# Attention row sums: all sixteen key tiles of a block summed on TensorE, behind the product with the values

## The reference

```
h = layer_norm(x) * scale + offset
q = (h @ wq) / sqrt(d);  k = h @ wk;  v = h @ wv          # 16 heads of width 32
q, k = rotary(q), rotary(k)
logits = einsum('bhik,bhjk->bhij', q, k)
a = softmax(logits, axis=-1)                              # over the 2048 keys j
y = einsum('bhij,bhjv->bhiv', a, v)
x = x + y @ wo
x = x + gelu(layer_norm(x) @ w1) @ w2
```

## Time and profile before

| | before |
|---|---|
| device time, median of 3 runs | 4409.26 us |
| device time, lowest and highest | 4403.0 and 4412.9 us |
| span of the profiled execution, first to last instruction | 4415.3 us |
| TensorE busy | 3909.2 us (89%) |
| VectorE busy | 2468.5 us (56%) |
| ScalarE busy | 1866.5 us (42%) |
| GpSimd busy | 2235.7 us (51%) |
| mean granted TensorE clock | 0.947 |

### The profile page before, as it was taken

How to read it: one execution, slowest core, us unless ns; L and a number is a source line. 1 busy time by engine, 2 the same in 40 slices (tenths; PEclk the granted TensorE clock), 3 DMA queues, 4 the chain that set the end, 5 groups by cost and what they waited for, 6 DMA issues and landing times. The chain is left out here.

```text
span 4415.3 us, 55170 instructions
## 1 busy us (share of the span) xinstructions
PE 3909.2 (89%) x19040; PEld 2452.9 (56%) x19040; DVE 2468.5 (56%) x3913; ACT 1866.5 (42%) x3553; POOL 2235.7 (51%) x1872
## 2 busy tenths in 40 slices
PE   5689999899899799899899996779989993997998
PEld 4545455355355354454454433668868882775776
DVE  4477878678787687877677763612211114333333
ACT  2246556556566466566565554321111112232222
POOL 0246767667677676777667774012212222343344
PEclk9889999999999899999999998889989996998999
DMA  6100000001000000000000003711110103011010
GB/s 211 59 17 25 18 20 20 9 25 28 9 23 18 16 25 22 11 27 8 22 23 8 3 6 115 249 61 48 49 58 20 58 29 131 15 48 38 27 55 19
DMA packets 103652, 184.72 MB, mean 42 GB/s; under 512 B 8976, under 2 KB 27920, under 8 KB 101136
## 3 DMA queue, kind: packets, MB, share of 16 engines
q1 hardware_dynamic: 103376, 181.15, 12.3%
HBM read 119.78 MB, written 61.08 MB: 41 GB/s over the span
## 5 line engine op out<-in xcount | busy, mean ns | idle before, releaser
L778 POOL TENSOR_TENSOR prob_sums<-prob_sums,probs 128x512 f32<-128x512 f32 x1152 | 1495.1, 1328 | 194.1 <-ACT probs L676 188.1
L580 DVE TENSOR_REDUCE part_max<-ps_att 128x1 f32<-128x512 f32 x2048 | 1316.7, 683 | 473.1 <-PE ps_att L463 459.5
L676 ACT ACTIVATE probs<-ps_att 128x512 f32<-128x512 f32 x2048 | 1130.1, 594 | 714.5 <-PE ps_att L445 670.2
L463 PE MATMUL ps_att<-k_stack,q_stack 96*128 96x512 f32 x2048 | 892.9, 440 | 102.0 <-DVE part_max L580 98.2
L445 PE MATMUL ps_att<-q_stack,k_stack 97*128 97x512 f32 x2048 | 897.7, 440 | 61.0 <-PEq L62 40.1
L445 PEld LDWEIGHTS ps_att<-q_stack,k_stack 97*128 97x128 f32 x2048 | 391.6, 192 | 499.9 <-ACT probs L676 376.5
L463 PEld LDWEIGHTS ps_att<-k_stack,q_stack 96*128 96x128 f32 x2048 | 401.6, 196 | 308.1 <-DVE part_max L580 221.6
L1209 POOL TENSOR_TENSOR ml_g_lo<-ml_g,ml_g_hi 128x512 fp32r<-128x512 f32 x128 | 164.9, 1288 | 788.6 <-DVE ml_g_hi L1185 788.6
L483 PE MATMUL ps_att<-probs,v_tok 128*32 128x512 f32 x4096 | 556.6, 616 | 2.3 <-ACT probs L676 2.3
L1185 DVE CAST ml_g_hi<-ml_g 128x512 fp32r<-128x512 f32 x128 | 54.7, 428 | 572.9 <-ACT ml_g L1145 572.9
L1145 ACT ACTIVATE ml_g<-ps_mlp 128x512 f32<-128x512 f32 x128 | 76.6, 599 | 586.9 <-PE ps_mlp L1224 586.9
(11 more groups left out here) (198 smaller groups left out, 5518.3 us busy)
## 6 DMA issues: line engine op xcount, KB each, us to landing
h_raw<-hS SPq DMA_DIRECT2D x128, 256.0 KB, 2.7
x_in_sb<-in_x SPq DMA_DIRECT2D x8, 1024.0 KB, 6.0
hS<-h_full SPq DMA_DIRECT2D x32, 256.0 KB, 2.8
yT<-o_sb SPq DMA_DIRECT2D x32, 256.0 KB, 2.1
po_x<-in_x SPq DMA_DIRECT2D x8, 1024.0 KB, 8.6
x<-po_x SPq DMA_DIRECT2D x8, 1024.0 KB, 6.6
h2T<-po_h SPq DMA_DIRECT2D x32, 256.0 KB, 2.1
ml_h<-h2T SPq DMA_DIRECT2D x32, 256.0 KB, 5.8
```

Source lines behind the costliest of these rows:

```text
L463: nc.tensor.matmul(mx[mx_uses % 2], t["qS"][0:S3, h, n * TB + q * P:n * TB + (q + 1) * P], t["kS"][0:S3, b, h, k * TB:(k + 1) * TB], start ...
L580: nc.vector.tensor_reduce(t["pm"][:, r, k:k + 1], mx[mx_uses % 2], AX.X, ALU.max)\
L676: nc.scalar.activation(t["p"][:, at % PR, h, :], sT[(at * G + h) % 2], ACT.Exp)\
L778: nc.gpsimd.tensor_tensor(t["acc"][:, h, :], x, t["p"][:, at % PR, h, :], ALU.add)\
```

## The change

All sixteen key tiles of a block are summed on TensorE, each right behind the product of the same tile with the values. The last matmul of tile 15 closes the sum. GpSimd has no additions of `probs` left; its other work stays. `last_sums` and the buffer `prob_sums` are gone. ScalarE waits, before it overwrites a `probs` buffer, for the sums of three steps ago and for nothing else, and copies the sums out right behind the values, in step 0 of the next block and not in step 2.

```diff
-POOL_SUMS = (0, 1, 2, 4, 5, 7, 8, 10, 11, 13, 14)
-PE_SUMS = tuple(k for k in range(LT) if k not in POOL_SUMS)
...
             def sums(w):
                 n, k = w // LT, w % LT
-                if k == PE_SUMS[0] and n:
+                if k == 0 and n:
                     pe.wait_ge(s["l_kept"], n)
                 for h in range(G):
                     mm = nc.tensor.matmul(l_ps[h * KD:(h + 1) * KD, :], c["ones"][:, 0:KD], t["p"][:, w % PR, h, :],
-                                          start=(k == PE_SUMS[0]), stop=False)
+                                          start=(k == 0), stop=(k == LT - 1))
                 mm.then_inc(s["psum"], 1)
...
                         if attend and at:
                             values(at - 1)
+                            sums(at - 1)
                         turn_stacks(st)
-                if attend and at and (at - 1) % LT in PE_SUMS:
-                    sums(at - 1)
-                if attend and at >= LT and k == 1:
-                    last_sums(at // LT - 1)
...
             def exps(at, heads):
                 for h in heads:
                     if at >= PR:
-                        v = at - PR
-                        if v % LT not in PE_SUMS:
-                            act.wait_ge(s["acc_done"], added(v, h))
-                        elif h == 0:
-                            act.wait_ge(s["psum"], summed(v))
                         if h == 0:
-                            act.wait_ge(s["pv"], v + 1)
+                            act.wait_ge(s["psum"], at - PR + 1)
...
             def keep_sums(n):
-                act.wait_ge(s["sum_done"], n + 1)
+                act.wait_ge(s["psum"], LT * (n + 1))
...
                 if attend and at >= LT and at % LT == 0:
                     keep_values(at // LT - 1)
-                if attend and at >= LT and at % LT == 2:
                     keep_sums(at // LT - 1)
...
-                if attend and st["k"] in POOL_SUMS and st["k"]:
-                    for h in range(G):
...
-                        nc.gpsimd.tensor_tensor(t["acc"][:, h, :], x, t["p"][:, at % PR, h, :], ALU.add)\
-                            .then_inc(s["acc_done"], 1)
```

More of the change, by code:

```diff
@@ L41 @@
 PR = 3
-POOL_SUMS = (0, 1, 2, 4, 5, 7, 8, 10, 11, 13, 14)
-PE_SUMS = tuple(k for k in range(LT) if k not in POOL_SUMS)
-POOL_ROUNDS = len(POOL_SUMS) - 1
 STEPS = NB * LT
@@ L341, in attend_groups @@
     blocks = len(halves) * NB if attend else 0
[L343 to L351, removed]
     ends = [(at + AHEAD) // (G * TT) for at, st in enumerate(steps)
@@ L493, in sums @@
                     mm = nc.tensor.matmul(l_ps[h * KD:(h + 1) * KD, :], c["ones"][:, 0:KD], t["p"][:, w % PR, h, :],
-                                          start=(k == PE_SUMS[0]), stop=False)
+                                          start=(k == 0), stop=(k == LT - 1))
                 mm.then_inc(s["psum"], 1)
-            def last_sums(n):
-                pe.wait_ge(s["acc_done"], G * POOL_ROUNDS * (n + 1))
-                for h in range(G):
-                    mm = nc.tensor.matmul(l_ps[h * KD:(h + 1) * KD, :], c["ones"][:, 0:KD], t["acc"][:, h, :],
-                                          start=False, stop=True)
-                mm.then_inc(s["sum_done"], 1)
             def turn_stacks(st):
@@ L566, in _ @@
                 sums(len(steps) - 1)
-                last_sums(blocks - 1)
         @block.vector
@@ L823, in attention @@
             hr=sb("h_raw", [P, 2, DC, P]),
-            p=sb("probs", [P, PR, G, TB]), acc=sb("prob_sums", [P, G, TB]),
+            p=sb("probs", [P, PR, G, TB]),
             k_stk=sb("k_stk", [P, 2, G * S3]), q_stk=sb("q_stk", [P, 2, G * S3]), ra=sb("rot_a", [P, 2 * P]),
@@ L830, in attention @@
         names = ("h_in0 h_in1 h_hi h_lo proj rot_cos rot_sin rotated v_kept k_hi q_hi k_split q_split turned k_kept q_kept "
-                 "w_in0 w_in1 w_hi w_lo mx_full mx_free neg_max max_set0 max_set1 score exp pv psum acc_done sum_done "
+                 "w_in0 w_in1 w_hi w_lo mx_full mx_free neg_max max_set0 max_set1 score exp pv psum "
                  "o_kept l_kept rl y_done y_stored ones_set")
```

## The result

The changed kernel takes 4521.8 us (median of 4 runs, 4520.1 to 4524.6) where the kernel before took 4410.6 us in the same job (4 runs, 4403.0 to 4412.9). The ratio is 1.0259, with a 95% interval of 1.0245 to 1.0274: 2.6% slower. Forecast were 4520 us and a range of 4475 to 4562.

The account below looks back on a forecast made before the run. Attention was taken as bound by TensorE's own order, with holes where VectorE is late. 277 us added less removed, minus 167 given back, minus 3, plus 4 makes 111 us on the 4409 us median: 4520 us, range 4475 to 4562.

Parts of the forecast that it names:

- What is added less what is removed: TensorE in attention: 512 sets of sums added, 450 us, less separate sets removed, 173 us: 277 us.
- The 0.88 us: TensorE's cost of one set of sums directly behind another set of the same shape, the values.
- The removed term: Separate sets at step ends: 70 at 1.2 us with a projection piece behind, 122 at 0.73 without: 173 us.
- What VectorE gives back: VectorE's instructions with two SBUF inputs, no longer slowed by GpSimd's additions, give back 167 us to TensorE.
- Its split: Of the 167 us: rotations 90, divisions 33, splitting the next weights 36, smaller ones 8.
- The waits: TensorE's waits for VectorE's reductions in attention were to fall from 292 to about 125 us.
- one of my own tests: Sign of being wrong: waits for VectorE fall by more than 250 us, the time then near the one before.
- Rival 1: VectorE's delays are not GpSimd's doing, or its remaining work holds VectorE just as long: 4620 us; chance 4%.
- Rival 2: Exponentials become the new wait, 0.3 us more in some 290 steps without a piece: 4607 us; chance 8%.
- Rival 3: The longer middle of a step absorbs all 291.8 us of waits for VectorE: 4371 us; chance 4%.
- The end of the last group: TensorE's wait of 3.4 us for GpSimd there goes.
- the copy of the sums in step 0: ScalarE's copy, about 0.6 us, delays exponentials; a wait of about 0.5 us in one block of a half, 4 us in all.

Follow-up runs that it names:

- the kernel without additions: Kernel before with GpSimd's additions left out (eleven of sixteen tiles missing from the sum), TensorE's order unchanged: 4248.0 us, ratio 0.9632.
- The kernel with its own sets in the middle: Kernel before with its own 5 + 1 sets of sums a block moved right behind the values, GpSimd's eleven tiles as before: 4375.2 us, ratio 0.9921.
- all sets at the end: Changed kernel with all sixteen sets of sums at the end of a step in place of behind the values: 4535.1 us, ratio 1.0287.
- The kernel nearest to that case: Changed kernel plus GpSimd's 40 additions a block on a private tile, with a second, different tile as other input: 4566.5 us, ratio 1.0348.
- the doubled tile: Changed kernel plus GpSimd's 40 additions a block, each adding one private tile to itself, read by nobody: 4539.5 us, ratio 1.0299.

## Why the prediction was right

The mechanism was right in the main: sets of sums on the bound engine at full price, and a part of it back because VectorE's instructions with two inputs are no longer held. The time was forecast within 2 us, which is better than its terms deserve: each of the two large ones was off by more, in opposite directions, and the split of the second is only in part confirmed. That much is luck.

- **What is added less what is removed** (277 us): 274 measured, as the changed kernel against the kernel without additions. The 0.88 us is in the trace of after. The removed term wasn't tested by itself. The kernel with its own sets in the middle took 4375 us where 4378 were expected, but in that sum the count of rotations was wrong; and all sets at the end cost 13 us where the same prices gave 26, so these prices are somewhat high.
- **What VectorE gives back** (167 us): 161 measured. The durations fell where they were said to, and the subtractions that GpSimd keeps do no harm (`q_rotated` 285 ns with 112 `k_stk` beside it).
- **Its split** (rotations 90, divisions 33, weights 36): the division alone gave 41. `q_rotated` alone gave 57, and `k_rotated` took up part of the rest. Since such gains overlap (132 us singly, 80 together), neither confirms its term closely. The weights were not tried alone, so their 36 is still an estimate. One instruction is missing from the split, the low part of the input tile, 112 times in attention:

```profile
L624 DVE TENSOR_TENSOR h_tile<-h_raw,h_tile 128x512 fp32r<-128x512 f32 x112 | 123.0, 1098 | 2.1 <-ACT h_tile L702 2.1
...
L598 DVE TENSOR_TENSOR h_tile<-h_raw,h_tile 128x512 fp32r<-128x512 f32 x112 | 76.4, 682 | 2.2 <-ACT h_tile L671 2.2
```

  The first row is before, the second after: 47 us of VectorE's time were given back here, as much as at the divisions (44). How much of it reached TensorE no run shows.

- **The waits**: wrong, and with them one of my own tests. I expected about 125 us of waits for the reductions to stay, by subtracting 167 from 292; 36 stayed. I had written that a fall by more than 250 us would bring the time near the one before. They fell by 255.5 us, and the time came out as forecast. The step that failed is the reading of a microsecond of shown wait as a microsecond of time: in the kernel without additions 291.8 - 32.6 = 259 us of waits went for 161 us of time, 0.62 each. It isn't a constant: the rotation on GpSimd gave 57 us for 112 us of waits, the division 41 for 56. Why it is less than one wasn't tested; part of a wait may only stand in the place of one for an exponential.
- **Rival 1** (VectorE not freed) was priced at 4620 us. The kernel nearest to that case took 4567: I let the sets cover 67 us of the delays, and they cover about 116, by the longer middle and whatever else differs there. It was refuted by the durations, as I had argued.
- **Rival 2** (exponentials become the new wait): no. Steps without pieces run mostly at 4.40 us, and the waits before score loads fell.
- **Rival 3** (the long middle absorbs everything): nearly all waits for VectorE did go, 255 of 292 us, and it was still 111 us slower, because a microsecond of wait was worth about 0.6 and the sets cost 274 us.
- **The end of the last group**: the wait of 3.4 us for GpSimd is gone, the copy of the sums in step 0 cost nothing that I could find. Neither was tested by itself.

## What to carry to other kernels

Work on an engine off the critical path isn't free: GpSimd, 51% busy and hardly waited for by anybody, cost this kernel 161 us, nearly all of it through VectorE. Taking the work off it still loses if the engine that is the bound then needs 274 us for it. Before work is moved, run the kernel with that work left out: it splits the change into its price and its gain. And where work must stand on the bound engine, try it where that engine would wait for another (here in the middle of a step), which was worth 34 us with the same work on each engine.

## What the runs showed of the hardware that wasn't expected

- A VectorE instruction with two inputs in SBUF can be held for as long as GpSimd adds without a pause. The division of 3.77 us (0.69 undisturbed) from 1467.32 to 1471.09 us ended 0.55 us after a round of four additions. In the kernel with its own sums in the middle one division, in the last block, was held for 34.06 us, beside a run of 28 additions, and it ended 0.5 us after the additions first paused, for 0.15 us. VectorE had nothing else to do in that stretch, so it held up nobody that the trace shows. First before, then that kernel:

```profile
1465.51 5.03 POOL L778 TENSOR_TENSOR prob_sums<-prob_sums,probs 128x512 f32<-128x512 f32 x4
```

```profile
2617.72 34.62 POOL L778 TENSOR_TENSOR prob_sums<-prob_sums,probs 128x512 f32<-128x512 f32 x28
...
2618.82 34.06 DVE L636 TENSOR_TENSOR o_sb<-o_sb,l_sb 128x512 f32<-128x512 f32 x1
...
2652.48 2.77 POOL L778 TENSOR_TENSOR prob_sums<-prob_sums,probs 128x512 f32<-128x512 f32 x2 [0.15 <-ACT probs L676]
```

- It need not be held that long. Before the change 14 of the 32 divisions took 1.58 to 1.63 us: they had their turn between two additions that followed each other at once. With the doubled tile (1074 ns an addition) no division took more than 1.33 us, although those additions follow each other at once too. What decides who is next, these runs don't show. A reciprocal, with one input, took 939 ns in attention with additions and 938 without. The Trainium skill, SBUF — State Buffer, section Who interferes with whom, speaks of a lock for the whole instruction, which fits the wait for an addition that is running.
- GpSimd's doubling of one tile (both inputs the same 128x512) took 1074 ns, with two different tiles 1318 ns.
